# A new order of work in the head and in the ten diffusion steps of a two-layer image kernel

## What is computed

```python
x = x + L0(_gn(x), ...)                      # _gn: group norm, 32 groups of 2 channels, per image
x = x + relu(conv3x3(_gn(x), w_q) + b)       # w_q: ternary weights, 64 -> 64 channels

# L0: an anisotropic diffusion of s0 in K = 5 steps
g  = relu(bn(depthwise3x3(h, wg)));  g1 = relu(bn(depthwise3x3(h, wg1)))
gy, gx = sobel(h)
Dx = 1/(gy*gy/4 + 1);  Dy = 1/(gx*gx/4 + 1)
ux = .5*(roll(g, 1, w) - roll(g, -1, w));  vy = .5*(roll(g1, 1, c) - roll(g1, -1, c))
# from these: D, E, c0, cm_x, cp_x, cm_y, cp_y, one value per element
for _ in range(5):
    prev = h
    h = D*(c0*h0 - 2*E*h + cm_x*roll(h,1,w) + cp_x*roll(h,-1,w) + cm_y*roll(h,1,c) + cp_y*roll(h,-1,c))
    h = h + D*(2*DT)*fsrc
    h0 = prev
return relu(bn(h))
```

## Time and profile before

| | us |
|---|---|
| median of 3 runs | 342.58 |
| lowest, highest of the 3 | 341.49, 476.98 |
| the profiled execution's own time | 342.63 |
| its span (first to last instruction) | 340.8 |
| busy in the span: PE / DVE / ACT | 263.7 / 270.2 / 137.7 |

### The profile page before, as it was taken

How to read it: one execution, slowest core, us unless ns; L and a number is a source line. 1 busy time by engine, 2 the same in 40 slices (tenths; PEclk the granted TensorE clock), 3 DMA queues, 4 the chain that set the end, 5 groups by cost and what they waited for, 6 DMA issues and landing times. The chain is left out here.

```text
span 340.8 us, 4181 instructions
## 1 busy us (share of the span) xinstructions
PE 263.7 (77%) x1754; PEld 235.0 (69%) x1754; DVE 270.2 (79%) x223; ACT 137.7 (40%) x198; POOL 2.8 (1%) x20
## 2 busy tenths in 40 slices
PE   0115899599979389999208999999999987768794
PEld 0114788488868377668108899999999976656583
DVE  1987259920399999939999999989999999997911
ACT  3248599984055142060203133242251040452843
POOL 1000000000000000000000000000000000000000
PEclk9999979969999989999757999999999999999899
DMA  7696000000000000000000000000030003000033
GB/s 255 160 430 260 0 2 2 0 0 2 0 0 2 0 0 2 0 0 2 0 0 0 2 0 2 2 0 2 0 125 4 0 0 125 2 0 0 0 125 123
DMA packets 4450, 13.87 MB, mean 41 GB/s; under 512 B 2256, under 2 KB 2256, under 8 KB 3536
## 3 DMA queue, kind: packets, MB, share of 16 engines
q1 hardware_dynamic: 4144, 12.88, 10.3%
q10 hardware_dynamic: 288, 0.72, 0.7%
HBM read 11.50 MB, written 2.10 MB: 40 GB/s over the span
## 5 line engine op out<-in xcount | busy, mean ns | idle before, releaser
L783 DVE TENSOR_TENSOR ring<-coef,state 128x2048 f32<-128x2048 f32 x56 | 124.4, 2286 | 9.2 <-ACT state L310 5.1
L1032 PE MATMUL psum<-mats,ring 128*128 128x128 f32 x896 | 102.9, 274 | 9.9 <-DVE ring L783 9.8
L1032 PEld LDWEIGHTS psum<-mats,ring 128*128 128x128 f32 x896 | 97.8, 141 | 13.5 <-DVE ring L783 13.4
L310 ACT ACTIVATE state<-psum 128x1024 f32<-128x1024 f32 x36 | 34.9, 1024 | 96.2 <-PE psum L1032 68.1
L992 PE MATMUL psum<-coef,state 128*128 128x256 f32 x192 | 45.4, 387 | 0.0
L992 PEld LDWEIGHTS psum<-coef,state 128*128 128x128 f32 x192 | 37.7, 196 | 5.4
L562 DVE SCALAR_TENSOR_TENSOR coef<-coef 128x2048 f32<-128x2048 f32 x15 | 34.4, 2290 | 0.5
L1032 PE MATMUL psum<-mats,first_two 128*128 128x128 f32 x64 | 11.0, 345 | 21.5 <-DVE first_two L562 21.5
L310 ACT ACTIVATE coef<-psum 128x512 f32<-128x512 f32 (+1 forms) x22 | 17.1, 785 | 26.2 <-PE psum L967 15.7
L967 PE MATMUL psum<-hi_s,sobel_m 128*128 128x512 f32 (+2 forms) x48 | 19.5, 412 | 9.4 <-DVE lo_s L625 7.5
L1032 PEld LDWEIGHTS psum<-mats,first_two 128*128 128x128 f32 x64 | 10.1, 185 | 22.1 <-issue 22.1
(11 more groups left out here) (121 smaller groups left out, 283.5 us busy)
## 6 DMA issues: line engine op xcount, KB each, us to landing
coef<-in_wide_taps SPq DMA_DIRECT2D x4, 1536.0 KB, 11.4
coef<-in_x SPq DMA_DIRECT2D x2, 1024.0 KB, 5.0
ring<-in_x SPq DMA_DIRECT2D x2, 512.0 KB, 6.7
ring<-in_x SPq DMA_DIRECT2D x1, 1024.0 KB, 9.8
out<-coef SPq DMA_DIRECT2D x2, 512.0 KB, 3.1
out<-coef SPq DMA_DIRECT2D x4, 256.0 KB, 2.9
mats<-in_matrices ACTq DMA_DIRECT2D x1, 384.0 KB, 6.6
bn<-in_norms ACTq DMA_DIRECT2D x1, 320.0 KB, 3.1
```

The lines of the kernel that those rows point to most:

```text
L310: return nc.scalar.activation(dst, src, func, **kw)
L783: V.tensor_tensor(wc(ring[:, slot, :]), wc(coef[:, t, a, :]), h_at(t, k, dw, dc), ALU.mult)\
L1032: ins = mm(slot_ap(name)[:, (j % 8) * 128:(j % 8) * 128 + 128], src[:, j * 128:j * 128 + 128], ident, is_transpose=True, start=first and j ...
```

## The change

No operation is added to or taken from the computation, apart from two small ones: the sum over tile 1 (`sum_x`) is made in two halves, and `mean_1` so comes from two matmuls. What changes is the place of the pieces in the queues and their slots.

- `ORDER` has the steps of tile 0 further ahead: (0,0) (1,0) (2,0) (0,1) (3,0) (1,1) (4,0) (2,1) (3,1) (4,1).
- At the end of the steps, `residual(0)` comes before step (3, 1) and not before (4, 1). `spread(0)`, `second_norm(0)` and `normalise(0)` stand in step (3, 1), then `lower_half(0, ·)`, and then the bare step (4, 1). PE makes `tx_0` in step (2, 1), `mean2_0` and `var2_0` in (3, 1), and `dense(0, 0)` between `add_source` and the products of (4, 1). `dense(0, 1)` follows in one piece.
- In the head of DVE: one half of the sum of tile 1 goes behind `sum_squares(0)`, the other into the wait for the reciprocal root; `split_lo(1)` goes behind `ternary`; the `alpha` part goes behind `source(0)`.
- In the head of ACT: `square_of(1)` behind the first Sobel square, the second `rsqrt_first` behind both `to_depthwise(0, ·)`, the Sobel squares of `gx_0` ahead of `scale_taps(6..8)`, `split_hi(1)` behind `wabs`, `reorder(1)` ahead of `to_natural(0, ·)`, `to_natural(0, 3)` ahead of `to_depthwise(1, ·)`. `reorder` reads in memory order and writes scattered; before, it read scattered and wrote in memory order.
- In the head of PE: `var_1` directly behind the two `gy_0` jobs, `depthwise(0, 3)` and `alpha` ahead of `to_depthwise(1, ·)`.

The diff, cut to its core:

```diff
-ORDER = [(0, 0), (1, 0), (0, 1), (2, 0), (1, 1), (3, 0), (2, 1), (4, 0), (3, 1), (4, 1)]
+ORDER = [(0, 0), (1, 0), (2, 0), (0, 1), (3, 0), (1, 1), (4, 0), (2, 1), (3, 1), (4, 1)]
...
-    early = ["mean_0", "var_0", "mean_1", "gy_0_0", "gy_0_1", "t2_0_0", "t2_0_1", "gx_0_0", "var_1", "gx_0_1",
-             "cv_0_0", "wsum", "cv_0_1", "cv_0_2", "t2_1_0", "t2_1_1", "cv_0_3"]
-    jobs = [(name, i % SLOTS) for i, name in enumerate(early)]
-    jobs += [("cv_1_0", 1), ("cv_1_1", 2), ("alpha", 3), ("gy_1_0", 0), ("gy_1_1", 3), ("gx_1_0", 0), ("gx_1_1", 3),
-             ("cv_1_2", 1), ("cv_1_3", 2)]
+    early = [("mean_0", 0), ("var_0", 1), ("mean_1", 2), ("gy_0_0", 3), ("gy_0_1", 0), ("var_1", 1), ("t2_0_0", 2),
+             ("t2_0_1", 3), ("gx_0_0", 0), ("gx_0_1", 1), ("cv_0_0", 2), ("wsum", 3), ("cv_0_1", 3), ("cv_0_2", 0),
+             ("cv_0_3", 1), ("alpha", 0), ("t2_1_0", 2), ("t2_1_1", 3), ("cv_1_0", 1), ("cv_1_1", 2), ("gy_1_0", 0),
+             ("gy_1_1", 3), ("gx_1_0", 0), ("gx_1_1", 3), ("cv_1_2", 1), ("cv_1_3", 2)]
+    jobs = list(early)
...
+        if (k, t) == (STEPS - 3, 1):
+            jobs += halves("tx", 0)
         if (k, t) == (STEPS - 2, 1):
-            jobs += halves("tx", 0)
+            jobs += [("mean2_0", 0), ("var2_0", 1)]
         if (k, t) == (STEPS - 1, 1):
-            jobs += [("mean2_0", 0), ("var2_0", 1), ("tx_1_0", 0), ("tx_1_1", 1)]
+            jobs += [("cf_0_0", 0), ("tx_1_0", 0), ("tx_1_1", 1)]
         jobs += halves(f"acc_{k}", t)
-    jobs += [("cf_0_0", 2), ("mean2_1", 0), ("var2_1", 1), ("cf_0_1", 3), ("tb_0_0", 0)]
-    quarter_slot = (2, 3, 0, 1)
+    jobs += [("cf_0_1", 2), ("mean2_1", 0), ("var2_1", 1), ("tb_0_0", 0)]
+    quarter_slot = (3, 2, 0, 1)
...
             def reorder(t):
-                copy(s_grouped[t].rearrange("p (g a w) -> p g a w", a=CP, w=W),
-                     h_at(t, 0).rearrange("p w (a g) -> p g a w", g=CG)).then_inc(s_reordered, 1)
+                copy(s_grouped[t].rearrange("p (g a w) -> p w a g", a=CP, w=W),
+                     h_at(t, 0).rearrange("p w (a g) -> p w a g", g=CG)).then_inc(s_reordered, 1)
...
             reorder(0)
-            square_of(1)
             scale_taps(range(4, 6))
             sobel_square(0, 0, 0)
+            square_of(1)
             sobel_square(0, 0, 1)
-            rsqrt_first(128, GROUPS)
             to_depthwise(0, 0)
             to_depthwise(0, 1)
+            rsqrt_first(128, GROUPS)
+            sobel_square(0, 1, 0)
+            sobel_square(0, 1, 1)
             scale_taps(range(6, 8))
-            sobel_square(0, 1, 0)
-            split_hi(1)
-            sobel_square(0, 1, 1)
             act.wait_ge(wl_in, 32)
             copy(wabs, wl, ACT.Abs, accum_out=wred[:, 0:1]).then_inc(wabs_ready, 1)
+            split_hi(1)
             scale_taps(range(8, 12))
             reciprocal_first(0)
             scale_taps(range(12, 16))
+            reorder(1)
             to_natural(0, 0)
             to_natural(0, 1)
-            reorder(1)
             wrap(0, 0, s_halo)
             d_of(0)
             to_natural(0, 2)
+            to_natural(0, 3)
             to_depthwise(1, 0)
             to_depthwise(1, 1)
-            to_natural(0, 3)
...
+                if (k, t) == (STEPS - 3, 1):
+                    rsqrt_first(128, BT)
+                    normalise(0)
+                    upper_half(0)
+            relu_dense(0, 0)
             relu_bn_out(1, 0)
             relu_bn_out(1, 1)
-            relu_dense(0, 0)
+            relu_dense(0, 1)
...
             sum_squares(0)
-            scale_s(0)
+            sum_x(1, 0)
+            scale_s(0, lambda: sum_x(1, 1))
...
             scale_s(1)
-            split_lo(1)
...
             denominator(0)
             ternary()
+            split_lo(1)
             newton(0)
             diffusivities(0)
+            divergence(0)
+            channels_made = over_channels(0)
+            g_made = scaled_g(0)
+            channels_made()
+            g_made()
+            source(0)
             wait_job(dve, "alpha")
...
             leave("alpha")
-            divergence(0)
-            channels_made = over_channels(0)
-            g_made = scaled_g(0)
-            channels_made()
-            g_made()
-            source(0)
...
-            for k, t in ORDER[2:-1]:
+            for k, t in ORDER[2:-2]:
                 step(k, t)
             residual(0)
-            step(STEPS - 1, 1, ((-1, lambda: spread(0)), (1, lambda: second_norm(0)), (3, lambda: normalise(0))))
+            step(STEPS - 2, 1, ((-1, lambda: spread(0)), (1, lambda: second_norm(0)), (3, lambda: normalise(0))))
             lower_half(0, 0)
             lower_half(0, 1)
+            step(STEPS - 1, 1)
             residual(1)
...
             sobel(0, 0, 1)
+            pe.wait_ge(vsum_ready, 2)
+            small("var_1", GROUPS, blockm, gsum[:, 1, 2, :])
             to_depthwise(0, 0)
             to_depthwise(0, 1)
             sobel(0, 1, 0)
-            pe.wait_ge(vsum_ready, 2)
-            small("var_1", GROUPS, blockm, gsum[:, 1, 2, :])
             sobel(0, 1, 1)
...
             depthwise(0, 2)
+            depthwise(0, 3)
+            pe.wait_ge(kept_ready, 1)
+            small("alpha", 2, ones[:, :], wred[:, 3:5])
             to_depthwise(1, 0)
             to_depthwise(1, 1)
-            depthwise(0, 3)
             depthwise(1, 0)
             depthwise(1, 1)
-            pe.wait_ge(kept_ready, 1)
-            small("alpha", 2, ones[:, :], wred[:, 3:5])
...
-                if (k, t) == (STEPS - 2, 1):
+                if (k, t) == (STEPS - 3, 1):
                     add_products(t, k, ((1, lambda: x_paired(0)),))
+                elif (k, t) == (STEPS - 2, 1):
+                    group_mean2(0)
+                    add_products(t, k, ((1, lambda: group_var2(0)),))
                 elif (k, t) == (STEPS - 1, 1):
-                    group_mean2(0)
-                    add_products(t, k, ((1, lambda: group_var2(0)), (4, lambda: x_paired(1))))
+                    pe.wait_ge(dense_m_ready, 6)
+                    dense(0, 0)
+                    add_products(t, k, ((4, lambda: x_paired(1)),))
...
-            pe.wait_ge(dense_m_ready, 6)
-            dense(0, 0)
+            dense(0, 1)
             group_mean2(1)
-            dense(0, 1, 0, 4)
             group_var2(1)
-            dense(0, 1, 4)
```

More of the change, by code:

```diff
@@ L517, in _ @@
                 wrap(t, k + 1, halo_ready)
-            rsqrt_first(128, BT)
-            normalise(0)
-            upper_half(0)
+                if (k, t) == (STEPS - 3, 1):
[3 more added lines that the diff above has]
+            relu_dense(0, 0)
             relu_bn_out(1, 0)
             relu_bn_out(1, 1)
-            relu_dense(0, 0)
+            relu_dense(0, 1)
             rsqrt_first(128, BT)
@@ L526, in _ @@
             upper_half(1)
-            relu_dense(0, 1)
             take_out(0, 0)
@@ L589, in grouped, with sum_x @@
                 return ap.rearrange("p w (g c) -> p w g c", c=2)
-            def sum_x(t):
-                for h in range(2 - t):
-                    dve.wait_ge((x_loaded[t], x_loaded0b)[h], 16)
-                    src = half(x_in[0], h) if t == 0 else x_in[1]
-                    V.tensor_reduce(gsum[:, t, (0, 4)[h], :], src.rearrange("p (w g c) -> p g w c", g=GROUPS, c=2),
-                                    AX.XY, ALU.add).then_inc(xsum_ready, 1)
+            def sum_x(t, h):
+                dve.wait_ge(x_loaded[t] if t or h == 0 else x_loaded0b, 16)
+                V.tensor_reduce(gsum[:, t, (0, 4)[h], :], half(x_in[t], h).rearrange("p (w g c) -> p g w c", g=GROUPS, c=2),
+                                AX.XY, ALU.add).then_inc(xsum_ready, 1)
             def mean_of(t):
@@ L612, in sum_squares, with scale_s @@
                                        AX.XY, ALU.add), vsum_ready, t + 1)
-            def scale_s(t):
+            def scale_s(t, meanwhile=lambda: None):
                 wait_job(dve, f"var_{t}")
-                ask = V.tensor_scalar(rs_in[:, 0:GROUPS], slot_ap(f"var_{t}")[:, 0:GROUPS], 1.0 / PER_GROUP, GN1_EPS,
-                                      ALU.mult, ALU.add)
-                rsqrt(128, GROUPS, gsum[:, t, 3, :], ask)
+                ask_rsqrt(V.tensor_scalar(rs_in[:, 0:GROUPS], slot_ap(f"var_{t}")[:, 0:GROUPS], 1.0 / PER_GROUP, GN1_EPS,
+                                          ALU.mult, ALU.add))
+                meanwhile()
+                rsqrt(128, GROUPS, gsum[:, t, 3, :])
                 s = grouped(h_at(t, 0))
@@ L630, in _ @@
             ask_rsqrt(V.tensor_scalar(rs_in[:, :], var, BN_EPS, None, ALU.add))
-            sum_x(0)
+            sum_x(0, 0)
+            sum_x(0, 1)
             rsqrt(128, NORMS, var)
@@ L645, in _ @@
                 .then_inc(shift_ready, 1)
-            sum_x(1)
             sum_squares(0)
-            scale_s(0)
+            sum_x(1, 0)
+            scale_s(0, lambda: sum_x(1, 1))
```

(11 more changed lines are left out.)

## The result

The changed kernel takes 356.88 us, the median of four runs (356.46 to 357.34). The kernel before, in the same comparison, takes 342.08. The ratio is 1.0449, with a 95% interval of 1.0425 to 1.0472: slower by 4.5%. The forecast was 354.0 within 348.5 to 358.0.

A forecast was written before the change was run, and what follows sets the result against it. No engine bounds throughout: slots and waits bind the head, PE the steps, DVE the end, PE the tail. 340.8 + 1.2 + 0.3 + 8.9 + 0.9 = 352.1, with 1.83 outside the span 354 us; range 348.5 to 358.

The forecast's parts named there:

- The head: Start to DVE's first product of the third step: `alpha` holding slot 0 delays tile 1's Sobel jobs; +1.2 us.
- From there on the old distances hold: After `gx_1_1` at 112.1, `depthwise(1, 2)` starts 2.2 later and two jobs take 11.5 us; PE free at 125.7.
- Group norm of tile 1: In the head: `s` of tile 1 comes at 45.4 as before, the reciprocal at 59.9.
- The reorder: In ACT's head: the new `reorder` costs between 2.0 and 4.1 us, covered by other waits.
- The steps: DVE's first product of the third step to `residual(0)`: 78.7 us, +0.3 beyond the one PE-bound step of 14.0 fewer.
- The last two steps: Steps (3,1) and (4,1), up to `residual(1)`: dependence and `dense(0, 0)` ahead of the products cost +8.9 us.
- The tail: From `residual(1)` to the end: order kept, 36.93 us, plus 0.9 for colder transposes on PE (0 to 2.5).
- Head gain stands: Rival: in the head, `source(0)`'s 13.8 us pass on if slot 0 doesn't hold tile 1's Sobel jobs; 341 us, chance 0.05.
- Dense hidden: Rival: the end of the steps is paced by DVE, so the price is 5.7 less; 348 us, chance 0.1.
- Something else in the head: Rival: a late slot or a wait priced too low in the head; 357 to 362 us, chance 0.1.
- PE colder: Rival: seven us of slow clock at the Sobel jobs, again at (2,0) and in the tail: 357; chance with forecast 0.75.
- the cold terms: Additions for PE at low clock: 2.8 us at tile 1's Sobel jobs, 0.9 in the tail; without them 350.

The follow-up runs named there:

- the first experiment: The kernel after with only the place of `dense(0, ·)` on PE, its slots and ACT's readers put back as before the change: 350.63 us, ratio 1.028.
- the second of two such moves on ACT: On the kernel with `to_natural(0, 2)` and `(0, 3)` ahead of `d_of(0)`, both `to_depthwise(1, ·)` put ahead of it too: 328.21 us, ratio 0.9614.
- the first by itself: On the new head with alpha part first and old steps, `to_natural(0, 2)` and `(0, 3)` put ahead of `d_of(0)` on ACT: 332.44 us, ratio 0.9712.

## Why the prediction was right, and where it was off

**The head.** The mechanism was right in each link. The `divergence` line was to come near 77 after some 6 us: 78.09 after 5.82. The Sobel jobs were to start at 99.2: 99.80. `gx_1_1` was to end at 112.1: DVE resumed at 112.04. Moving the alpha part back gave 9.7 us, so the place of the alpha part, which holds the slot, is the cause. The sum was 1.6 short. The step that failed is "From there on the old distances hold": `depthwise(1, 2)` and `(1, 3)` took 13.0 us and not 11.5 (114.12 to 127.10), since the clock fell again, so DVE's fourth product came at 130.79 and not at 129.2. Three smaller misses stand in the timelines: the reciprocal came at 60.6 and not at 59.9, the Sobel jobs 0.6 late, and the cold Sobel stretch cost 2.0 where I put 2.8, which hid a part of the miss behind it.

**Group norm of tile 1.** I had it at 45.4 as before; it came at 47.0. `to_depthwise(0, 1)` on ACT, with the reciprocal root behind it, waited for transposes at the low clock:

```profile
38.70 0.41 PE L935 MATMUL psum<-gsum,mats 128*128 128x32 f32 x2 [2.35 <-DVE gsum L611]
38.95 3.30 PE L941 MATMUL psum<-mats,ring 128*128 128x128 f32 x16
```

They took 3.30 us for 16, where 1.91 is usual. I hadn't priced the 2.35 us of idle time in front of them.

**The reorder.** I had left its price open between 2.0 and 4.1, without effect. It is 3.77 and 3.82 us (4.10 before), with ACT waiting for other work behind it both times. So scattering the writes costs nearly what gathering the reads does. The Trainium skill says in "SBUF — State Buffer", in the note on cachelines under "Door 1: The DMA port swizzle", that each access that crosses to a new 16-byte line pays. The trace agrees for either side: both forms have one side in steps of more than 16 bytes, and neither comes near the 1.91 us of a plain copy of this size.

**The steps.** 79.40 against 78.7. The miss is the start of (2,0). PE had stood for 15.38 us, and its first sums ran at the low clock, as the stretch from 187 to 192 shows:

```profile
187.00:192.00 5.00, 4.82 (x23) 4.82 (x24) 5.00 (x4) 0.00 (x0) 0.00 (x0) 0.50 0.00 0
```

PE ended (2,0) at 200.5, 15.7 us after DVE's first product, where I had 15.1. The rest of the steps is PE-bound and carries that on. I had this in the range, not in the sum.

**The last two steps.** 46.28 against 44.9. The dense job is worth 4.6 us of it by its own experiment. The term that was too small is again the clock: PE is idle for 3.86 us while DVE normalises tile 0, and the last sum of (3,1) took 2.92 us and not 1.97, the transposes behind it 2.66 and not 1.97. Before, `x_paired(1)` stood in this place and filled the pause to 2.17 us, and what came behind it was hidden under `lower_half` and `residual(1)`.

**The tail.** I had put 0.9 us on a colder start; the tail took 36.80 us and not 37.8. PE's first transposes were indeed slow (1.97 us for eight, 1.09 before), but the low clock also ended earlier behind them: after two and a half dense matmuls, not eight. But this is no rule of the tail. The kernel after with the alpha part moved back, and the one with more work for PE, have the same tail with the same pause of 6.57 us in front of it, and took 38.2 and 38.3 us. The stretches at the same place, first in the kernel after and then in the one with the alpha part moved back, where everything comes 10.4 us earlier:

```profile
334.00:336.00 2.00, 2.00 (x9) 1.90 (x8) 1.48 (x2) 1.16 (x2) 0.00 (x0) 0.50 0.00 0
336.00:338.00 2.00, 2.00 (x9) 1.60 (x9) 1.58 (x2) 0.52 (x1) 0.00 (x0) 0.92 0.11 43
```

```profile
324.00:326.00 2.00, 2.00 (x8) 1.81 (x8) 1.71 (x2) 1.17 (x2) 0.00 (x0) 0.50 0.00 0
326.00:328.00 2.00, 2.00 (x6) 1.52 (x6) 1.18 (x2) 0.12 (x1) 0.00 (x0) 0.50 0.31 125
```

There the low clock lasted over nine dense matmuls. So a fixed price for the cold start is the step that failed: behind one and the same pause it differs by 1.4 us between executions, and 0.9 lies within that. The -1.0 of the tail is luck, and it offset misses elsewhere: with 38.2 the span would have been 356.0 and the time 357.9, just inside the stated range. Why the low clock ended sooner in one execution stays open.

**The rivals.** "Head gain stands" fell: of 13.8 us nothing arrived, as `gx_1_1` came at 112. "Dense hidden" fell by the first experiment. "Something else in the head" (357 to 362) didn't come; the head was 1.6 over its sum. "PE colder" is what happened in the head, in the steps and in the last two steps, within the range: the span is 2.5 us over the forecast, of which 1.6 in the head, 0.7 and 1.4 in the steps, and -1.0 in the tail, less 0.1 in `residual(0)`, with 0.1 of rounding.

The sentence on the Trainium skill, "TensorE: Matmul & The Clock Gate", Part 1, has its answer too. The first statement fits what the kernel after shows behind its long pauses (6.58, 7.54, 15.38, 3.86 and 6.57 us): the matmuls start at the low clock and come out of it while PE works. The second, that the ramp is under 1% of a typical span, is true of one pause here (2.0 us of 354.6 by the experiment), but with the cold terms left out the sum would have been 350, further from the measured 356.9 than the 354 with them. A price that is small against a span isn't small against the differences that such a change is about.

## What to carry to other kernels

When a short instruction that frees a buffer is moved behind long ones, ask which queue takes that buffer next, and what that queue's work is holding up: here a part of DVE's queue that is busy for 0.4 us, behind 21 us of other work, stopped PE, and PE's job stopped DVE. When a job is moved forward in the queue of an engine, put it where that engine waits for a *late* partner, not where its work just becomes ready, as `dense(0, 0)` did in front of the sums of (4,1); a gap on the timeline of before is only free if nothing in the new order fills it. And after taking a wait away, look for the next one in the same queue before judging the move: the second of two such moves on ACT was worth 4.2 us, the first by itself 1.5, which isn't clear of the noise.

## What the runs showed of the hardware

The granted clock of TensorE was what the forecast missed by in the head, in both parts of the steps and in the tail. Pauses of 2.18 us and 2.35 us were followed by slow matmuls in the kernel after (4.44 us for twelve that take 2.75, 3.30 us for 16 that take 1.91), and so was one of 15.38 us. But the very same pause of 2.18 us in front of `depthwise(1, 2)` stands in eleven of the traces, and in four of them (the kernel before among them) the twelve matmuls took 2.75 us, in the other seven 4.04 to 4.44. By the length of the pause alone the price can't be told from these runs. It varies from execution to execution at the end, too. With the kernel before's order of the dense jobs the tail took 35.3 to 35.4 us in three traces and 36.9 to 37.0 in five, and with the new order 36.8 in one and 38.2 to 38.3 in two. These steps of some 1.5 us are as large as some of the effects that were looked for here, and more runs are needed for those. No run fills the pause in front of the tail, so that this pause is what brings the low clock there isn't shown.
